# Dense matmuls of no use and DMA buffers on multiples of 512 bytes in a graph layer with routed experts

## The reference

```
xl = layernorm(x)
agg = segment_sum(xl[dst], src)          # 53125 edges
y = agg + w * xl
h = relu(relu(relu(y @ W1.T) @ W2.T) @ W3.T)      # 256 -> 64 -> 32 -> 256
x = x + h + xl
t = layernorm(x); t = layernorm(t) * gamma + beta
logits = t @ Wr + br                     # 8 experts
top two of the logits, softmax of the two
x = x + sum over the two of weight * (gelu(t @ W1[e] + b1[e]) @ W2[e] + b2[e])
```

## Time and profile before

| | us |
|---|---|
| median of 3 runs | 470.71 |
| the 3 runs | 469.35 to 474.88 |
| profiled execution, its own time | 475.65 |
| its span, first to last instruction | 473.7 |
| mean granted TensorE clock in it | 0.867 |
| PE busy | 403.2 |
| DVE busy | 297.0 |
| ACT busy | 221.7 |

### The profile page before, as it was taken

One profiled execution on the slowest core, in us unless ns is written; L12 is line 12 of the kernel. 1 busy time (PEld: TensorE's weight loads), 2 busy tenths in 40 slices (PEclk: granted clock), 3 DMA queues, 4 the chain that ended last, 5 costly groups with the idle time before them and its releaser, 6 DMA issues.

```text
span 473.7 us, 13144 instructions
## 1 busy us (share of the span) xinstructions
PE 403.2 (85%) x4382; PEld 357.1 (75%) x4383; DVE 297.0 (63%) x717; ACT 221.7 (47%) x351; POOL 135.3 (29%) x241
## 2 busy tenths in 40 slices
PE   7898779999999688997045999999999999999910
PEld 4696578999999556666034999999999999999900
DVE  5963998999993735355886444444444444454893
ACT  3455467788888127555003544444444444444300
POOL 3320000000000050000006565665665665664210
PEclk9855589999999959787555999999999999999965
DMA  8710099999999829991002122222222222248688
GB/s 200 169 42 1 13 190 160 207 209 208 208 209 210 124 56 344 350 322 55 0 1 68 56 69 75 72 66 68 74 69 76 68 66 67 76 120 221 161 228 271
DMA packets 112699, 62.17 MB, mean 131 GB/s; under 512 B 86626, under 2 KB 106744, under 8 KB 112545
## 3 DMA queue, kind: packets, MB, share of 16 engines
q1 hardware_dynamic: 101014, 41.58, 39.1%
q0 software_dynamic: 6272, 14.93, 10.3%
q10 hardware_dynamic: 5386, 5.33, 4.0%
HBM read 27.70 MB, written 13.64 MB: 87 GB/s over the span
## 4 chain that ended last, share of the span: by engine, by line
PE 69%; DVE 9%; DMA 6%; ACT 5%; issue 4%; SPq 4%; ACTq 1%; DVEq 0%; POOLq 0%
PE psum L954 19%; PE psum L965 18%; PE psum L822 9%; PE psum L813 7%; DMA at<-cts 4%; PE psum L873 3%; PE psum L747 3%; PE psum L895 2%; PE psum L943 2%; DMA w_sb<-pair_rows 2%; SPq L389 2%; SPq L415 1%; PE psum L738 1%; PE psum L863 1%; ACTq L290 1%
## 5 line engine op out<-in xcount | busy, mean ns | idle before, releaser
L954 PE MATMUL psum<-xgT,w_now 128*128 128x128 f32 x832 | 103.2, 278 | 0.3 <-DVE xgT L1389 0.3
L954 PEld LDWEIGHTS psum<-xgT,w_now 128*128 128x128 f32 x832 | 98.7, 195 | 0.7 <-issue 0.7
L965 PE MATMUL psum<-w_sb,hT 128*128 x416 | 98.5, 380 | 0.1
L607 ACT CAST cts<-psum 128x1000 bf16<-128x1000 f32 x100 | 78.6, 815 | 26.7 <-PE psum L813 25.9
L965 PEld LDWEIGHTS psum<-w_sb,hT 128*128 128x128 f32 x416 | 75.1, 190 | 8.5 <-issue 0.5
L822 PE MATMUL psum<-z,at 125*128 (+1 forms) x1875 | 73.0, 195 | 7.5 <-DMA at<-cts 7.2
L695 ACT ACTIVATE hT<-up 128x512 f32<-128x512 f32 x52 | 32.8, 630 | 98.7 <-DVE up L1398 98.7
L822 PEld LDWEIGHTS psum<-z,at 125*128 125x128 bf16 x1875 | 66.3, 99 | 10.5 <-DMA at<-cts 6.0
L684 ACT COPY w_now<-w_sb 128x1024 f32 x52 | 54.4, 1046 | 34.3 <-DVEq L1346 21.9
L497 POOL DMA_INDIRECT pair_rows<-yb,scol x52 | 51.7, 994 | 47.4 <-issue 34.0
L1398 DVE TENSOR_TENSOR up<-psum,b1T 128x512 f32<-128x512 f32 x52 | 35.9, 691 | 45.1 <-PE psum L954 45.1
(11 more groups left out here) (237 smaller groups left out, 383.1 us busy)
## 6 DMA issues: line engine op xcount, KB each, us to landing
w_sb<-in_L_ffn_W_dram SPq DMA_DIRECT2D x2, 4096.0 KB, 20.0
token_rows<-tok SPq DMA_DIRECT2D x5, 560.0 KB
tok<-pair_rows SPq DMA_DIRECT2D x5, 560.0 KB
w_sb<-pair_rows SPq DMA_DIRECT2D x5, 560.0 KB
out_dram<-res ACTq DMA_DIRECT2D x5, 560.0 KB
res<-in_x_dram ACTq DMA_DIRECT2D x3, 560.0 KB
res<-in_x_dram SPq DMA_DIRECT2D x2, 560.0 KB
b_sb<-in_L_ffn_b_dram SPq DMA_DIRECT2D x1, 1024.0 KB, 23.5
```

The lines of the kernel that those rows point to most:

```text
L607: act.copy(cts[:, par, :, d0:d0 + nw * WD].rearrange("p h (b d) -> p b h d", b=nb), psum[:, bank:bank + nb, 0:wb * WC].rearrange("p b (d h ...
L954: last = pe.matmul(psum[:, j % 2, c * P:(c + 1) * P], w1_now[:, j % 2, k, c * P:(c + 1) * P], xgT[:, j % 2, k, :], start=(k == 0), stop=(k ...
L965: last = pe.matmul(psum[:, 4 + j % 2, 0:D], hT[:, j % 2, k, :], w2_sb[:, ds(e, 1), k, :].rearrange("p a h -> p (a h)"), start=(k == 0), st ...
```

## The change

And PE gets more matmuls of no use, at five places:

```diff
+        IDLE_BANK = (7, 1, 2, 4, 0)
...
             def first_layer(g):
                 for i, (t0, t1) in enumerate(PAIRS):
                     pe.wait_ge(xT_sb, g * len(PAIRS) + i + 1)
+                    if g >= 1:
+                        keep_going(2, IDLE_BANK[g], 0)
...
             turn_weights()
+            pe.wait_ge(z_sb, 2 * G)
             first_layer(4)
...
-                keep_going(4, 3, F1)
+                keep_going(10, 3, F1)
                 pe.wait_ge(keyT_sb, (r + 1) * 4)
...
                 for kt in (NT - 2, NT - 1):
                     for c in range(NC):
+                        if c % 2 == 0:
+                            keep_going(4, 3, F1)
                         apply(kt, kt // NBUF, kt % NBUF, c)
...
+            keep_going(10, 6, 0)
             pe.wait_ge(L["few"], 80)
+
+            def keep_at_it(n):
+
+                for _ in range(n):
+                    pe.matmul(psum[:, 3, 3 * P:4 * P], later[:], later[:], start=False, stop=True, skip_group_check=True)
...
                     last.then_inc(tokT_psum, 1)
+                    if g == 0 and t == 0:
+                        pe.wait_ge(bias_sb, 1)
+                    if g < NG - 1:
+                        keep_at_it(3)
...
                         last = pe.matmul(psum[0:T, 3, c:c + NX], tokT[:, k, t, :], wr_gam[:, k, :], start=(k == 0), stop=(k == KD - 1))
+                    if t < G - 1:
+                        keep_at_it(2)
                 last.then_inc(logit_psum, 1)
```

More of the change, by code:

```diff
@@ L80, in build @@
         pair_dram = nc.dram_tensor("pair_rows", [2 * N + NB * P, D], F32, kind="Internal").ap()
+        sb("gap_res", [P, 96], F32)
         res = sb("res", [T, NT, D], F32)
@@ L166, in build @@
         fin_half, fin_done, out_stored = sem("fin_half"), sem("fin_done"), sem("out_stored")
+        sb("gap_early", [P, 88], F32)
         early = ExitStack()
+        at = sb("at", [P, NBUF, NT, P], BF16, early)
+        sb("gap_at", [P, 64], F32, early)
+        cts = sb("cts", [P, NBUF, NT, P], BF16, early)
+        sb("gap_cts", [P, 64], F32, early)
+        gath = sb("gath", [T, NG, CH, 2], F32, early)
         start_f = sb("start_f", [T, NG + 1], F32, early)
         start_i = sb("start_i", [T, NG], I32, early)
-        gath = sb("gath", [T, NG, CH, 2], F32, early)
         keyT = sb("keyT", [P, 2, NW, 2], BF16, early)
@@ L184, in build @@
         gW3_sb = sb("gW3_sb", [P, 2, F2], F32, early)
-        at = sb("at", [P, NBUF, NT, P], BF16, early)
+        sb("gap_prep", [P, 104], F32, early)
         prep = ExitStack()
@@ L208, in build @@
         prep.close()
+        oh_lo = sb("oh_lo", [P, NBUF, NQ, P], BF16, early)
         oh_col = sb("oh_col", [P, NBUF, NQ, WC2], BF16, early)
-        oh_lo = sb("oh_lo", [P, NBUF, NQ, P], BF16, early)
-        cts = sb("cts", [P, NBUF, NT, P], BF16, early)
         early.close()
@@ L219, in build @@
         b2_sb = sb("b2_sb", [P, NX, D], F32, lt)
+        tok = sb("tok", [T, NT, D], F32, lt)
+        xg = sb("xg", [P, 4, D], F32, lt)
+        yb = sb("yb", [P, 4, D], F32, lt)
+        tot = sb("tot", [P, NX, NT], F32, lt)
+        blk = sb("blk", [P, 4, NX], F32, lt)
         gidx = sb("gidx", [P, NB], I32, lt)
@@ L223, in build @@
         quads_i = sb("quads_i", [1, 1], I32, lt)
-        tok = sb("tok", [T, NT, D], F32, lt)
         mlp = ExitStack()
@@ L240, in build @@
         sel = sb("sel", [T, NT, NX], BF16, route)
-        tot = sb("tot", [P, NX, NT], F32, route)
-        blk = sb("blk", [P, 4, NX], F32, route)
         pos = sb("pos", [T, 2, NT], F32, route)
@@ L261, in build @@
         scol = sb("scol", [P, 4], I32, lt)
-        xg = sb("xg", [P, 4, D], F32, lt)
         xgT = sb("xgT", [P, 2, KD, P], F32, lt)
@@ L266, in build @@
         hT = sb("hT", [P, 2, KH, P], F32, lt)
-        yb = sb("yb", [P, 4, D], F32, lt)
         lt.close()
```

## The result

The changed kernel takes 456.76 us (median of 4 runs, 453.77 to 459.25) against 471.78 for the kernel before beside it: ratio 0.968, 95% interval 0.959 to 0.976. Run once more in a later series it took 458.53 (6 runs) against 468.43, ratio 0.985 (0.980 to 0.990). The runs of the kernel before scatter by 463 to 481 us over all series; the size of the gain is thus 10 to 15 us, its sign is clear. The forecast of 462.5 was too high, and 456.76 lies just outside the range. All numbers by stage are of one profiled execution of each kernel, for the changed one that of 456.44.

The account below looks back on a forecast made before the run. PE at half clock was taken to bound the first and small layers, DVE the adjacency. From 475.65, −6.3 − 0.4 − 0.7 − 3.2 − 3.3 + 0 = −13.9 gave 461.7; plus 0.8, 462.5 us, range 457 to 470.5.

## What to carry to other kernels

Before calling an engine the bound, compare its pace in a stretch with the pace that its own list gives without waits (here 3.94 against 3.58 us a tile for DVE, which was busy 18.70 of 20 us): a single microsecond shows too little, and a busy share near 1 hides waits shorter than an instruction's drawn tail. In a software pipeline look at the latency of the longest transfer against the distance at which its result is used, and at the spacing of the landings against the time of a tile; if either is tight, a landing 0.8 us shorter, here by 160 bytes of padding ahead of one buffer, is worth several us, here 6.9 against 8.4 in the medians for 156 matmuls of no use. And where the clock falls at places that differ from run to run, price a filler by several profiles of the kernel before, not by one.

## What was not expected of the hardware

- A transposing DMA with source rows of 256 bytes lands in 3.5 to 3.6 us (median) with the rows at offset 0 or 256, and in 4.3 at 32 or 352; the offset of its destination (0 or 384) does not matter. Its issue on SP takes 1.53 to 1.56 us (medians of the aligned profiles) against 1.70 to 1.84. The two of a tile, issued one behind the other, land 1.6 us apart, against 2.0.
- The granted clock falls at different places in profiles of one kernel: group 4's third layer took 4.09 in one and 2.40 in another. In the first layer it fell between 18 and 21 us in five profiles of twelve in spite of the fillers and was back at 1.00 by 31 us, where without them it stayed at 0.50 to 48 us.
